# Routed expert results: from a plain store and late gathers to scatters in the loop and plain loads

## What is computed

```
for i in range(2): shared += ffn(xf, sw1[i], sw2[i], sw3[i])   # two shared experts
logits = xf @ router_w.T + expert_bias                         # 8 experts
rw, sel = top_k(logits, 2); rw = softmax(rw)
out = shared + sum over the two chosen e: rw_e * ffn(xf, w1[e], w3[e], w2[e])
ffn(x, a, b, c) = (silu(x @ a.T) * (x @ b.T)) @ c.T            # hidden width 512
```

## Time and profile before

| | us |
|---|---|
| median of 3 runs | 1105.44 (1102.66 to 1107.54) |
| the profiled execution | 1107.57 |
| its span in the profile | 1105.6 |

### The profile page before, as it was taken

One profiled execution on the slowest core, in us unless ns is written; L12 is line 12 of the kernel. 1 busy time (PEld: TensorE's weight loads), 2 busy tenths in 40 slices (PEclk: granted clock), 3 DMA queues, 4 the chain that ended last, 5 costly groups with the idle time before them and its releaser, 6 DMA issues. The chain is left out here.

```text
span 1105.6 us, 19661 instructions
## 1 busy us (share of the span) xinstructions
PE 1026.7 (93%) x7166; PEld 954.2 (86%) x7166; DVE 702.8 (64%) x1651; ACT 514.0 (46%) x1061; POOL 399.4 (36%) x645
## 2 busy tenths in 40 slices
PE   5999998599799999995999999999999999999983
PEld 4899998488799999995877889999999999999982
DVE  5577776366588888883657545544445666666762
ACT  4446665323466666662244533333344444444441
POOL 5324455407223332222732100000004867767540
PEclk9999999599999999997999999999999999999995
DMA  7200000201377778883311310000000111111000
GB/s 217 77 1 1 1 1 1 76 1 58 102 208 238 235 237 239 236 223 114 95 39 58 115 29 1 20 1 1 1 1 11 22 28 30 30 30 29 11 10 10
DMA packets 57529, 78.54 MB, mean 71 GB/s; under 512 B 5680, under 2 KB 37552, under 8 KB 57456
## 3 DMA queue, kind: packets, MB, share of 16 engines
q1 hardware_dynamic: 38896, 50.04, 15.1%
q0 software_dynamic: 16304, 24.91, 8.2%
q10 hardware_dynamic: 2256, 2.62, 0.7%
HBM read 62.61 MB, written 14.94 MB: 70 GB/s over the span
## 5 line engine op out<-in xcount | busy, mean ns | idle before, releaser
L40 PE MATMUL bank<-V_hi,XT_lo 128*128 128x256 f32 x416 | 123.6, 297 | 1.2 <-DVE XT_lo L2001 1.2
L2001 DVE TENSOR_TENSOR XT_lo<-bank,XT_lo 128x512 fp32r<-128x512 f32 x116 | 73.3, 633 | 77.8 <-ACT XT_lo L1694 77.2
L1694 ACT ACTIVATE XT_lo<-bank 128x512 fp32r<-128x512 f32 x116 | 63.9, 553 | 119.0 <-PE bank L1453 118.4
L42 PE MATMUL bank<-V_hi,XT_lo 128*128 128x256 f32 x416 | 117.1, 281 | 0.0
L41 PE MATMUL bank<-V_lo,XT_lo 128*128 128x256 f32 x416 | 116.9, 281 | 0.0
L40 PE MATMUL bank<-rx_hi,expert_w_hi 128*128 128x256 f32 x368 | 106.4, 289 | 2.5 <-PEq L846 2.5
L42 PE MATMUL bank<-rx_hi,expert_w_lo 128*128 128x256 f32 x368 | 104.7, 284 | 0.0
L41 PE MATMUL bank<-rx_lo,expert_w_hi 128*128 128x256 f32 x368 | 104.5, 284 | 0.0
L2006 DVE TENSOR_REDUCE part<-wide 128x1 f32<-128x402 f32 (+1 forms) x116 | 72.4, 624 | 38.7 <-PE wide L42 36.7
L406 DVE TENSOR_TENSOR expert_w_lo<-sraw,expert_w_hi 128x1024 fp32r<-128x1024 f32 x72 | 88.0, 1222 | 13.4 <-ACT expert_w_hi L402 13.3
L40 PE MATMUL wide<-expert_w_hi,XT_hi 128*128 128x402 f32 (+1 forms) x232 | 91.4, 394 | 3.4 <-issue 2.4
(11 more groups left out here) (414 smaller groups left out, 3302.9 us busy)
## 6 DMA issues: line engine op xcount, KB each, us to landing
sraw<-w1T SPq DMA_DIRECT2D x25, 512.0 KB, 5.4
sraw<-w3T SPq DMA_DIRECT2D x25, 512.0 KB, 5.1
sraw<-w2T SPq DMA_DIRECT2D x25, 512.0 KB, 3.9
routed_results<-rys POOLq DMA_DIRECT2D x23, 256.0 KB, 4.4
XT_hi<-queries POOLq DMA_DIRECT2D x16, 256.0 KB, 3.3
X<-x ACTq DMA_DIRECT2D x4, 512.0 KB, 7.5
token_rows<-Fx SPq DMA_DIRECT2D x4, 512.0 KB, 4.9
out<-X SPq DMA_DIRECT2D x16, 128.0 KB, 1.7
```

Of the source, the lines that this page charges most:

```text
L40: pe.matmul(out, wh, xh, start=first, stop=False)
L42: return pe.matmul(out, wl, xh, start=False, stop=last)
L1694: act.activation(weights(g, nk, 0), transposed(g, nk), ACT.Copy).then_inc(sem["high"], 1)
L2001: dve.tensor_tensor(weights(g, nk, 1), transposed(g, nk), weights(g, nk, 0).bitcast(F32), ALU.subtract).then_inc(sem["low"], 1)
```

## The change

- The lists are made with token numbers 1 to 2048 for first choices and 2049 to 4096 for second ones (`ids`), so one list serves twice: as `back_lists` (0 for an empty place) for where a result goes, and, taken modulo 2048, as `lists` for which token to fetch. Empty places fetch token row 2047 now (row 0 before) and send their result to row 0 of a new DRAM tensor, which nobody reads.
- In the routed loop POOL no longer stores a tile's 256 rows with one plain DMA; it scatters them by two indirect DMAs of 128 rows, a gather of 128 rows behind each. Each scatter waits until all scatters before it have landed.
- The last tile's result is copied into `raw`, and its two scatters are issued at the start of the second shared expert.
- In the second shared expert the 32 gathers are gone. SyncE waits for all 46 scatters, then issues nine plain loads of the rows in token order, and then the six weight loads. POOL is left with the two scatters and `inverse`.
- DVE adds the first half of a block's routed rows in chunk 3 and the second half in chunk 0 of the next block (chunks 2 and 3 before), but for the last block, which is as before.

```diff
 RT = 256
 NR = (2 * S + E * (RT - 1)) // RT
+NL = RT // P * (NR + 1)
...
+                def load_back(sp, b):
+
+                    def load(dst, k, i, n):
+                        r = 1 + k * S + i * P
+                        sp.dma_start(dst.rearrange("p (i d) -> p i d", d=D),
+                                     rows_back[r:r + n * P, :].rearrange("(i p) d -> p i d", p=P)).then_inc(gathered[b], 16)
+                    i, n = b * TB, TB
+                    load(first_back[:, i * D:(i + n) * D], 0, i, n)
+                    n = min(n, NC - i)
+                    load(second_back[:, i * D:(i + n) * D], 1, i, n)
+                    if n < TB:
+                        load(rest[:, 0:(TB - n) * D], 1, i + n, TB - n)
+
                 @blk.sync
                 def _(sp):
+                    sp.wait_ge(stored_results, 16 * RT // P * NR)
+                    for b in range(NB):
+                        load_back(sp, b)
...
-                    def gather(b):
-                        for i in range(b * TB, (b + 1) * TB):
-                            for k in range(2):
-                                pool.indirect_dma_start(back(k, i), None, rows_out[:, :],
-                                                        bass.IndirectOffsetOnAxis(ap=pos[:, k, i:i + 1], axis=0))\
-                                    .then_inc(gathered[b], 16)
-
                     def inverse(b):
...
                         pool.tensor_scalar(h, h, -1.0, None, ALU.mult).then_inc(inv, 1)
+                    for t in range(RT // P):
+                        scatter_back(pool, NR - 1, t, raw[:, 0:RT // P * D], rows_back, back_lists)
                     for b in range(NB - 1):
-                        gather(b)
-                    inverse(0)
-                    gather(NB - 1)
-                    for b in range(1, NB - 1):
                         inverse(b)
...
                     def add_routed(b, h):
 
-                        dve.wait_ge(gathered[b], 16 * 2 * TB)
+                        dve.wait_ge(gathered[b], 16 * (2 if (b + 1) * TB <= NC else 3))
                         for k in range(2):
...
+                            if b and c == 0:
+                                add_routed(b - 1, 1)
                             if b and c == 1:
                                 add_result(b - 1)
...
-                            if c >= 2:
+                            if b == NB - 1 and c >= 2:
                                 add_routed(b, c - 2)
+                            elif b < NB - 1 and c == 3:
+                                add_routed(b, 0)
...
+        def scatter_back(pool, j, t, src, rows_back, back_lists):
+
+            n = RT // P * j + t
+            if n:
+                pool.wait_ge(stored_results, 16 * n)
+            pool.indirect_dma_start(rows_back[:, :], bass.IndirectOffsetOnAxis(ap=back_lists[:, n:n + 1], axis=0),
+                                    src[:, t * D:(t + 1) * D], None).then_inc(stored_results, 16)
...
-            rows_out = nc.dram_tensor("routed_results", (NR * RT, D), F32, kind="Internal").ap()
+            rows_back = nc.dram_tensor("results_by_token", (1 + 2 * S, D), F32, kind="Internal").ap()
...
-                def gather(pool, j):
+                def gather(pool, j, halves=(0, 1)):
 
                     if j >= 2:
                         pool.wait_ge(td, j + 1)
-                    for t in range(RB):
+                    for t in halves:
...
-                        pool.iota(ids_i, pattern=[[P, NT]], base=0, channel_multiplier=1).then_inc(made, 1)
+                        pool.iota(ids_i.rearrange("p (k i) -> p k i", k=2), pattern=[[S, 2], [P, NT]], base=1,
+                                  channel_multiplier=1).then_inc(made, 1)
...
                             dve.wait_ge(listing, 1)
-                            dve.tensor_copy(lists[:, :], spare[:, 0:NL]).then_inc(listed, 1)
+                            link(dve.tensor_scalar(list_u[:, :], spare[:, 0:NL], float(S - 1), None, ALU.add))
+                            dve.tensor_copy(back_lists[:, :], spare[:, 0:NL])
+                            dve.tensor_scalar(lists[:, :], list_u[:, :], S - 1, None, ALU.bitwise_and).then_inc(listed, 1)
...
-                        for j in range(NR):
+                        for j in range(NR - 1):
+                            if j:
+                                pool.wait_ge(stored_results, 16 * RB * j)
+                                pool.sem_inc(ysf, 1)
                             pool.wait_ge(ye, j + 1 + 1)
-                            pool.dma_start(rows_out[j * RT:(j + 1) * RT, :].rearrange("(t p) d -> p t d", p=P),
-                                           ys[:, j % 2, :].rearrange("p (t d) -> p t d", d=D)).then_inc(stored_results, 16)
+                            scatter_back(pool, j, 0, ys[:, j % 2, :], rows_back, back_lists)
                             if j + 4 <= NR:
-                                gather(pool, j + 4)
-                            pool.wait_ge(stored_results, 16 * (j + 1))
-                            pool.sem_inc(ysf, 1)
+                                gather(pool, j + 4, (0,))
+                            scatter_back(pool, j, 1, ys[:, j % 2, :], rows_back, back_lists)
+                            if j + 4 <= NR:
+                                gather(pool, j + 4, (1,))
+                        pool.wait_ge(stored_results, 16 * RB * (NR - 1))
+                        pool.sem_inc(ysf, 1)
 
...
-                        def results(j, par):
+                        def results(j, dst):
                             dve.wait_ge(yd, j + 1)
                             dve.wait_ge(ysf, j + 1)
-                            dve.tensor_copy(ys[:, par, :].rearrange("p (t d) -> p t d", d=D),
+                            dve.tensor_copy(dst.rearrange("p (t d) -> p t d", d=D),
...
-                                results(j - 1, 1 - par)
+                                results(j - 1, ys[:, 1 - par, :])
...
-                        results(NR - 1, 0)
+                        results(NR - 1, raw[:, 0:RB * D])
```

28 lines of the change are left out of this document (13 added, 15 removed).

## The result

| | before | after |
|---|---|---|
| median of the runs compared (us) | 1104.05 (1102.54 to 1107.54) | 1114.46 (1113.47 to 1116.31) |
| span of the profiled execution | 1105.6 | 1114.3 |
| ratio, 95% interval | | 1.0089 (1.0068 to 1.011) |

The account below looks back on a forecast made before the run. TensorE, busy 93% of the span, was taken as the bound. The terms -4.4 + 0 - 0.3 + 0.3 + 0.2 = -4.2 us gave 1101.2 us from the runs' median of 1105.44; range 1097 to 1109.

Parts of the forecast that it names:

- Part 1: Second shared expert: without the gathers queued ahead, GpSimd's first inverse starts earlier and TensorE's stall goes; gain 4.4 us.
- Part 2: Routed loop: each tile's two serial scatters take 7.6 us, under the tile's 8.92, so they cost nothing.
- The rival: Routed loop: the scatter chain outruns the tile, from a mean landing of 4.3 us; 1118 us in all; chance 0.18.
- an estimate of 4.8 us for a serial scatter: Routed loop: landing of 2.8 plus 2 us of HBM latency under load; the sum would be some 1123 us.
- Part 3: Last six scatters, of empty tiles 20 to 22: writing 128 times to one row adds 1.0 us each.
- Part 4: Between loop and second expert: GpSimd's drain grows to 7.3 us for 88 DMAs, yet TensorE restarts 0.3 us earlier.
- Part 5: Start of second expert: loads behind the scatters bring the first weight 25.0 us after TensorE's start; cost 0.3 us.
- the limit of 24.2: Second expert: latest arrival of the first weight, in us after TensorE's start, without TensorE noticing.
- the charge of 0.3: Second expert: us charged for the first weight exceeding its latest harmless arrival by 0.8 us.
- part 6: Before the first gather: two more small VectorE instructions for the lists cost 0.2 us.

Follow-up runs that it names:

- the kernel without waits: The changed kernel with empty places scattered to separate rows behind the buffer, and no scatter waiting for the one before: 0.9952 of the kernel before.
- own rows: The changed kernel with empty places scattered to separate rows behind the buffer instead of all to row 0: 0.9992 of the kernel before.
- the kernel at the old addresses: The changed kernel with unused SBUF (256 and 192 bytes per partition), weights and hidden tile placed modulo 512 as before the change: 1.0051 of the kernel before.
- the scattering one: The changed kernel with separate rows for empty places, no scatter waits, reordered loads, five drains in the loop, placement modulo 512 as before: 0.9883, 1092.36 us.

## Why the prediction was wrong

- **Part 1, the gathers out: right.** 4.4 us by the profiles, with the 2.7 of the medians beside it (above). After's own rows show the cause gone: GpSimd takes up the inverse as soon as the statistics are there.

```profile
558.88 0.38 DVE L272 BATCH_NORM_AGGREGATE MV<-stats 128x2 f32<-128x6 f32 x4
```

```profile
559.36 0.23 POOL L173 TENSOR_SCALAR RSTD<-MV 128x4 f32<-128x4 f32 x1 [26.10 <-DVE MV L272]
```

- **Part 2, the chain under the tile: the step that failed.** The prediction had 3.9 + 0.3 + 3.1 + 0.3 = 7.6, under the tile of 8.92, and charged the loop nothing; measured are 3.72 + 0.34 + 4.77 + 0.87 = 9.69, over it. That 3.72 is near 3.9 is luck: it is a mean of landings of 2.4 to 2.9 and of 3.8 to 5.6. Too low was the landing beside the weight loads. Where the first scatter starts as foretold, 0.9 us ahead of a w3 load, it takes 5.2 in tile 0, and 5.42 in all 20 tiles of the kernel without waits, whose second ones take 3.06, close to the 3.1. With 5.2 for the first, the second starts just ahead of the w2 load and takes 4.53; "the second scatter falls where the weight loads pause" fell with the 3.9, and from tile 2 on it is the first that falls there, at best. The last term was 0.87, since the release of the buffer and two waits stand between the landing and the next issue. The rival named this mechanism, and its threshold of 4.3 us against a measured mean of 4.25; with the 0.6 us of steps between that neither counted, it was crossed. I had given it 0.18. I took the low value from gathers alone on the DMA engines when the rows of the loop itself said 4.5. Its price of 1118 was on the high side, since the chain catches the pause again now and then. The prediction also worked out an estimate of 4.8 us for a serial scatter from the Trainium skill ("DMA: Bandwidth & Descriptors", Latency and other measured facts); the runs show 4.98 beside loads and 2.61 in their pause. The 1123 that it gives by that is too low by its own terms: 20 times 1.3 less 6, and 5 for the lag at the end, make 1126.
- **Part 3, one row for all: right in kind, sized at the wrong place.** The four scatters of the two empty tiles in the loop land in 3.1 us each. With own rows the scatters away from the weight loads land in 2.4 to 2.5: 0.7 instead of 1.0. But I charged them only at the loop's end. A nearly empty scatter inside the loop paid 1.4, and a chain without reserve loses its step by that. The landings, first of those four, then of five with own rows (tiles 20, 21 and the first of 22, of which tile 20's two, near the last loads, make the 3.1):

```profile
DMA to landing us min/median/max: 3.1/3.1/3.1
```

```profile
DMA to landing us min/median/max: 2.4/2.5/3.1
```

  The Trainium skill says of a repeated destination ("DMA: Bandwidth & Descriptors", Rules for kernel authors) that each duplicate's write goes out on its own and one lands. It gives no time for that. The 0.7 us are this case's; whose data stays no run here shows.
- **Part 4, the drain: right.** 7236 ns for 88 DMAs, 7.3 foretold. The line through the counts doesn't hold for few: 517 for 2, 119 for the 1 since the drain before. TensorE's restart came 10 us after its last matmul all the same, since the scatters ended later.
- **Part 5, the loads behind the scatters: right on when the weight comes, too low in its charge.** The first split came 25.7 us after TensorE's start (25.0), 5.54 us after ScalarE was free, and TensorE stood 2.2 us:

```profile
552.46 0.63 ACT L206 ACTIVATE expert_w_hi<-sraw 128x512 fp32r<-128x512 f32 x1 [5.54 <-DMA sraw<-L_xattn_Wq_cT]
```

  It came 1.5 past the limit of 24.2, and ScalarE's second silu behind it 1.8 later after TensorE's start than before (560.92 less 526.74, against 548.74 less 516.38). So the charge of 0.3 should have been about 1.8: past a limit, each tenth counts in full. The last scatter took 4.50 us, 0.7 more than charged; the same scatter took 3.12 in the kernel at the old addresses, so the row isn't why, and the cause is open.
- **Not in the sum at all:** 3.9 us by which the result matmuls got slower through other addresses. Nothing in the trace of before could have told it; the diff could, since it moved an allocation.

The sum of -4.2 with what was measured: part 1 -4.4, loop +11.2 (of which an estimated 3.9 the addresses) for 0, idle between the blocks +0.5 for -0.3, loads +1.8 for +0.3, and, of no known cause, -1.4 ahead of the loop, within what this stretch varies by, and +1.0 behind the second expert: +8.7. The 0.2 of part 6 can't be told from that -1.4.

## What to carry to other kernels

A wait for a landing inside a loop makes a chain of all its landings, priced beside the loop's own loads, plus every step between; compare that sum with the loop's period. Here 8.9 us in a period of 9.07 left next to nothing for a late step, and a scatter of 1.4 us more was enough to lose the step in the trace shown. Send what nobody reads to places of its own, above all where later transfers wait for it. And when a block ends in a GpSimd drain on the path, drain it earlier, beside other work: that gave 0.6% here.

## What the runs showed of the hardware that I had not expected

- Scatters of 128 KB take 2.61 us in the pause of the weight loads and 4.98 beside them (43 and 77 scatters). With the first scatter and a gather of their own queue still under way, 20 of them took 3.06 in the pause, so the loads of another queue weigh more than what goes ahead in their own.
- 128 writes to one row instead of 128 rows: 0.7 us more without other traffic (3.1 against 2.4). In the loop 1.4 more for one nearly empty scatter in the pause, and -0.6 to +0.6 for three wholly empty ones beside the loads.
- Result matmuls of 256 columns come 113, 118 or 120 ns apart at the full clock, in four placements of weights and hidden tile in SBUF (120 in two of them), the same in every trace of a placement.
- GpSimd's drain at a block's end, with all its DMAs landed, takes 5.5 us for 67, 7.2 for 88, some 2.7 for 32 and 2.0 for 24: 0.08 us for each; 0.52 for 2, and 0.12 for 1. The first four inside the loop took 2.3 to 4.0 us in the kernel before and 10.7 to 10.9 in the scattering one; where landings are recorded, they end 0.5 to 1.0 us behind the last one, of DMAs issued after the drain's start too. Beside TensorE's work that cost nothing.
- The kernel before takes 1.5% longer in some sets; in its variants profiled in one of them ScalarE, VectorE and TensorE stand idle beside GpSimd's gathers, for up to 23, 21 and 12 us at a time. There the change is faster.
